# Moving five pieces of side work between the places of an attention turn: one projection in two halves, two transposes into one place, one more projection in two halves

## The chip, the cores and the metric

The kernel runs on one core of a Trainium2 chip. The metric is the device time of one launch in microseconds (us). The five engines of the core appear under their profile names: PE (TensorE, with its weight loads as PEld), DVE (VectorE), ACT (ScalarE), POOL (GpSimd) and SP (SyncE, which here only issues DMAs).

## The reference

A layer of attention and a mixture of experts, both modulated by a condition vector, over 4 batches of 512 tokens of width 256, all in float32.

```python
h = _layernorm(x) * (1 + ca) + sa
x = x + ga * _L0_attn_ref(h, wq, wk, wv, wo)      # 16 heads of 16, softmax over 512 keys
h = _layernorm(x) * (1 + cb) + sb
x = x + gb * _L0_ffn_ref(h, ...)                  # 32 experts of 96, top 4 of 32, plus a shared expert of 512
```

## The kernel before

**Stages.** After a short lead (loads, first projections, maxima of the first scores) come four attention turns, one for each batch (t.b = 0 to 3), then the rest of the second batch-wise work (`finish`), then the experts in 48 pairs of tiles, then the sums. The change touches the turns alone.

**A turn** has 32 *places*, 8 for each of 4 groups of 4 heads. At each place PE issues first the **score block**: two transposed score matmuls (`scoreT`, L863), whose exponentials ACT takes (L691), and two plain score matmuls (`score`, L834) of a later group, whose row maxima DVE takes (L1201). After the block comes `between`, the side work of the place. At every even place `between` begins with `values` (L876), the product of the exponentials and V, for a four of units. The remaining side work is laid out by hand in the tables `FIRST` (turn 0), `MIDDLE` (turns 1 and 2) and `LAST` (turn 3): name and place, or two places where a job is issued in two halves.

**The jobs** that matter here:
- `QK0` to `QK3` (L812) project the next batch's queries (even numbers) and keys (odd). A whole one is two matmuls, one for each half of the contraction; PE's records count four. ACT copies the result to `qk_raw` (L588), and SP spreads it to `q_rows` or `k_rows` by 8 DMAs (L356).
- `MAX0` to `MAX3` (L842) transpose the collected maxima of a group. ACT writes their negative to `neg_max` (L606), and SP puts that into a row of `q_rows` by 4 DMAs (L364). The next group's `scoreT` needs it, at the next place that is a multiple of 8.
- `HT0`, `HT1` (L798, inputs `h_even` or `h_odd`) are four transposes each of the previous batch's second normalisation. ACT writes them to `h2T` (L631) with scale and bias.
- `V0`, `V1` (L821), `WO0`, `WO1` (L889), `LOG` (L919), `RANK`, `NT0`, `NT1` are the rest.

**One side bank.** In turns 0 to 2 every one of these jobs writes the same PSUM bank (semaphores misc0_full and misc0_free). `claim` lets PE start a job only when the reader of the job before it has freed the bank; so the order of names in the table is the order of uses of the bank. ACT and DVE do their parts in their own `between`, after the two exponentials or maxima of that same place. There are three banks for transposed scores and three for plain ones, so the second `scoreT` of a block waits for an exponential of the block before, and the second `score` for a maximum of it.

Of the kernel before, what the change touches and what calls it, by code (L numbers as in the profile page):

```python
# [52 lines left out]
class Turn:  # L53
# [4 lines left out]
    LEAD = ("TP0", "TP1", "QK0", "QK1", "QK2", "QK3", "V0", "V1", "MAX3")  # L58

    FIRST = {"MAX0": 0, "TP0": 1, "TP1": 3, "QK0": 5, "QK1": 7, "MAX1": 8, "MOD0": 9, "MOD1": 11, "V0": (13, 15),  # L60
             "MAX2": 16, "MODT": 17, "QK2": (19, 21), "QK3": 23, "MAX3": 24, "V1": (27, 29), "NT0": 30, "NT1": 31}

    MIDDLE = {"MAX0": 0, "QK0": 1, "WO0": 3, "WO1": 5, "MAX1": 8, "QK1": 9, "V0": (11, 13), "HT0": 14, "HT1": 15,
              "MAX2": 16, "LOG": 17, "QK2": (19, 21), "QK3": 23, "MAX3": 24, "RANK": 25, "V1": (27, 29), "NT0": 30, "NT1": 31}

    LAST = {"MAX0": 0, "WO0": 3, "WO1": 5, "MAX1": 8, "HT0": 12, "HT1": 13, "LOG": 15, "MAX2": 16, "RANK": 20}
# [85 lines left out]
def adaln_moe_kernel(nc, x_in, wq, wk, wv, wo, gate, up, down, sgate, sup, sdown, c_in, wmod_in, out):  # L152
    ctx = ExitStack()
    with ctx:
# [403 lines left out]
        def _(act):  # L558
# [22 lines left out]
            def raw_qk(t, c):  # L581

                src = full(act, t, f"QK{c}")
                if c == 0:

                    for g in range(NG):
                        above(act, rows_ld[g], 128 * (t.b + 1))
                frees(act.activation(qk_raw[:, c, :], src, ACT.Copy), t, f"QK{c}")  # L588
# [12 lines left out]
            def negate_max(t, g):  # L601

                src = full(act, t, f"MAX{g}")

                above(act, maxrow, 64 * (NG * t.b + g + 1))
                frees(act.activation(neg_max[:, :], src[0:TJ * G, 0:P], ACT.Copy, scale=-1.0), t, f"MAX{g}")  # L606
# [49 lines left out]

            def between(t, place):

                if t.att and place % 8 == 0 and (place < 24 or t.pre):
                    negate_max(t, place // 8)  # L660
                for k in range(KD):
                    if t.at(f"TP{k}", place):
                        to_hT(t, f"TP{k}", t.b + 1)
                    if t.at(f"NT{k}", place):
                        to_hT(t, f"NT{k}", t.b + 2)
                    if t.at(f"V{k}", place):
                        values_out(t, k)
                    if t.at(f"HT{k}", place):
                        h2T_out(t, k)
                for c in range(4):  # L670
                    if t.at(f"QK{c}", place):
                        raw_qk(t, c)
                if t.next and place in (18, 20, 22, 26):
                    normalise(turn_of[t.b + 1], [(18, 20, 22, 26).index(place)])
                if t.post:
                    norms = t.WHEN_LAST["NORM"] if t.fill else t.WHEN["NORM"]
                    if place in norms:
                        second_norm(t, [j for j in range(TJ) if norms[j] == place])
                    if t.at("LOG", place):
                        logits_out(t)  # L680
                    if t.now("EXPS", place):
                        expert_weights(t)
# [92 lines left out]
        def _(pe):  # L775
# [61 lines left out]
            def turn_max(t, g):  # L837


                pe.wait_ge(max_done, 64 * t.b + 16 * g + 32)  # L840
                bank = claim(t, f"MAX{g}")
                filled(pe.transpose(bank[0:TJ * G, 0:P], max_q[:, (g + 1) % 2, :, :].rearrange("p q i -> p (q i)"), ident[:, :]), t, f"MAX{g}")  # L842
# [120 lines left out]
            def between(t, place):  # L963

                g = place // 8
                if place % 2 == 0:
                    if place % 8:
                        values(t.b, g, place // 2 % 4 - 1)
                    elif g or t.post:
                        values(t.b if g else t.b - 1, (g - 1) % NG, TJ - 1)  # L970
                if place % 8 == 0 and (g < 3 or t.pre):
                    turn_max(t, g)
                for k in range(KD):
                    if t.at(f"TP{k}", place):
                        tokens_to_columns(t, f"TP{k}", t.b + 1)
                    if t.at(f"NT{k}", place):
                        tokens_to_columns(t, f"NT{k}", t.b + 2)
                    if t.halves(f"V{k}", place):
                        project_v(t, k, t.halves(f"V{k}", place))
                    if t.at(f"MOD{k}", place):  # L980
                        modulate(t, k)
                    if t.at(f"WO{k}", place):
                        project_o(t, k)
                    if t.at(f"HT{k}", place):
                        pe.wait_ge(h2_norm, TJ * t.b)
                        rows_to_columns(t, f"HT{k}", h2[(t.b - 1) % 2], k)
                for c in range(4):
                    if t.halves(f"QK{c}", place):
                        project_qk(t, c, t.halves(f"QK{c}", place))
                if t.at("MODT", place):  # L990
                    modulation_columns(t)
                if t.at("LOG", place):
                    logits(t)
                if t.at("RANK", place):
                    ranks(t)
# [644 lines left out]
```

## Time and profile before

| | us |
|---|---|
| median of 3 runs | 603.67 (603.39 to 603.87) |
| the profiled execution | 604.01 |
| its span in the trace | 602.2 |

What lies around the span is 604.01 - 602.2 = 1.8 us. A row of the chain of waits gives a start, a length and what ran; it says what each moment of the end time was spent on. A block that runs unhindered is four pieces of 0.63, 0.01, 0.42 and 0.01 us in that view. In a row of the timeline the length is that of the merged instructions, and the bracket behind it says how long the engine sat idle before them and for whom. The turns lie between about 49 and 333 us.

### The profile page before, as it was taken

The numbers are of one execution on the slowest core, as the hardware profiler recorded it, in microseconds if no ns is written. First come the engines' busy times: TensorE is split into PE (matmuls) and PEld (weight loads), VectorE is DVE, ScalarE is ACT, GpSimd is POOL, SyncE is SP. The second block draws the span as 40 slices with busy tenths as digits, with TensorE's granted clock in tenths as the row PEclk, the third lists the DMA queues.
The fourth block names the chain that finished last, engine by engine and source line by source line (L and its number), as shares of the span: only waits on it lengthen the run. The fifth ranks groups of instructions, "written<-read, shape, count | busy, mean of one in ns | idle before, by whom it ended". The sixth has DMA issues, their size and how long they took to land.

```text
span 602.2 us, 10736 instructions
## 1 busy us (share of the span) xinstructions
PE 563.6 (94%) x3118; PEld 313.8 (52%) x3119; DVE 370.8 (62%) x860; ACT 255.3 (42%) x519; POOL 217.8 (36%) x284
## 2 busy tenths in 40 slices
PE   4889999999999999999999999998999999999881
PEld 3443233333333333333343465668888898897570
DVE  6385677778589785898855569435444444443683
ACT  3113545564765647555568140022343443433000
POOL 6100000000110751108434653441675666667332
PEclk9966999999999999999999999999999999999996
DMA  7242126100501224012101169524555645540791
GB/s 227 42 132 97 34 54 188 37 11 10 115 4 34 93 70 115 7 31 90 53 1 41 66 267 330 147 82 130 158 157 151 182 144 165 166 124 9 269 371 58
DMA packets 42343, 67.18 MB, mean 112 GB/s; under 512 B 9291, under 2 KB 32212, under 8 KB 41948
## 3 DMA queue, kind: packets, MB, share of 16 engines
q1 hardware_dynamic: 30208, 45.62, 25.9%
q0 software_dynamic: 7680, 16.87, 8.2%
q10 hardware_dynamic: 4416, 4.20, 2.1%
q8 instruction: 21, 0.34, 0.2%
q14 instruction: 18, 0.15, 0.1%
HBM read 38.93 MB, written 27.51 MB: 110 GB/s over the span
## 4 chain that ended last, share of the span: by engine, by line
PE 81%; DVE 8%; issue 3%; DMA 3%; SPq 1%; ACT 1%; POOL 1%; ACTq 0%; POOLq 0%; DVEq 0%
PE ps L863 23%; PE ps L876 10%; PE ps L1089 9%; PE ps L1110 6%; PE ps L960 6%; PE ps L812 5%; PE ps L954 3%; PE ps L834 3%; PE ps L1075 3%; PE ps L821 3%; PE ps L889 3%; DVE max_q L1201 2%; PE ps L1100 2%; PE ps L798 2%; PE ps L919 1%
## 5 line engine op out<-in xcount | busy, mean ns | idle before, releaser
L1201 DVE TENSOR_REDUCE max_q<-ps 128x1 f32<-128x512 f32 x256 | 163.8, 686 | 74.5 <-PE ps L834 72.8
L691 ACT ACTIVATE probs<-ps 128x512 f32<-128x512 f32 x256 | 138.0, 596 | 99.5 <-PE ps L863 99.2
L834 PE MATMUL ps<-k_rows,q_rows 31*128 31x512 f32 x512 | 149.7, 678 | 1.8 <-DMA k_rows<-qk_raw 1.8
L863 PE MATMUL ps<-q_rows,k_rows 32*128 32x512 f32 x512 | 147.6, 646 | 0.9 <-DVE max_q L1201 0.9
L545 POOL DMA_INDIRECT results<-y_sb,dest x96 | 94.5, 984 | 64.8 <-issue 35.0
L863 PEld LDWEIGHTS ps<-q_rows,k_rows 32*128 32x128 f32 x512 | 42.9, 186 | 71.6 <-ACT probs L691 52.2
L1089 PE MATMUL ps<-up_sb,oT 128*128 x384 | 70.7, 328 | 1.5 <-DVE oT L1565 1.3
L876 PE MATMUL ps<-probs,v_ext 128*32 128x512 f32 x512 | 68.2, 605 | 1.1 <-ACT probs L691 1.1
L1089 PEld LDWEIGHTS ps<-up_sb,oT 128*128 128x128 f32 x384 | 61.4, 191 | 2.1 <-issue 1.9
L1110 PE MATMUL ps<-down_sb,e_hidT 96*128 x192 | 49.8, 383 | 3.8 <-ACT e_hidT L748 3.8
L498 POOL TENSOR_TENSOR rstd<-veps,mhalf 128x4 f32<-128x4 f32 x4 | 4.1, 1036 | 134.3 <-DVE veps L1283 132.4
L1565 DVE COPY oT<-ps 128x512 f32<-128x512 f32 x48 | 33.1, 691 | 30.0 <-PE ps L1075 30.0
L834 PEld LDWEIGHTS ps<-k_rows,q_rows 31*128 31x128 f32 x512 | 46.0, 194 | 10.5 <-DVE max_q L1201 3.9
L1572 DVE CAST dest<-xe 128x2 int32<-128x2 f32 x48 | 14.8, 309 | 48.4 <-ACT e_silu L731 46.5
L731 ACT ACTIVATE e_silu<-ps 128x192 f32<-128x192 f32 x48 | 15.8, 330 | 63.6 <-PE ps L1089 63.6
L740 ACT ACTIVATE y_sb<-ps 128x512 f32<-128x512 f32 x48 | 28.7, 597 | 29.2 <-PE ps L1110 27.0
L1110 PEld LDWEIGHTS ps<-down_sb,e_hidT 96*128 96x128 f32 x192 | 32.7, 190 | 7.7 <-issue 5.1
L876 PEld LDWEIGHTS ps<-probs,v_ext 128*32 128x32 f32 x512 | 10.1, 108 | 49.8 <-issue 31.1
L644 ACT ACTIVATE sh_tanh<-ps 128x512 f32<-128x512 f32 x16 | 9.6, 597 | 61.5 <-PE ps L960 61.5
L525 POOL DMA_INDIRECT dispatched<-h_even,slot_i x32 | 31.4, 983 | 9.5 <-POOL h_even L524 9.5
L525 POOL DMA_INDIRECT dispatched<-h_odd,slot_i x32 | 31.1, 972 | 9.1 <-POOL h_odd L524 9.1
L1075 PE MATMUL ps<-ident,xe 128*128 128x128 f32 x192 | 29.0, 273 | 0.8 <-DMA xe<-dispatched 0.8
(180 smaller groups left out, 695.7 us busy)
## 6 DMA issues: line engine op xcount, KB each, us to landing
xe<-dispatched SPq DMA_DIRECT2D x96, 129.0 KB, 2.1
up_sb<-results SPq DMA_DIRECT2D x16, 512.0 KB, 7.9
up_sb<-in_up SPq DMA_DIRECT2D x2, 3072.0 KB, 15.1
dispatched<-pad_rows SPq DMA_DIRECT2D x33, 129.0 KB, 4.5
down_sb<-in_down SPq DMA_DIRECT2D x1, 3072.0 KB, 31.3
x<-in_x ACTq DMA_DIRECT2D x4, 512.0 KB, 5.1
q_rows<-qk_raw SPq DMA_DIRECT2D x64, 32.0 KB, 1.9
k_rows<-qk_raw SPq DMA_DIRECT2D x64, 32.0 KB, 1.9
```

The lines of the kernel that those rows point to most:

```text
L525: pool.indirect_dma_start(out=xs, out_offset=bass.IndirectOffsetOnAxis(ap=slot_i[:, TOPK * j + k:TOPK * j + k + 1], axis=0), in_=h2[p % 2] ...
L545: pool.indirect_dma_start(out=yk, out_offset=bass.IndirectOffsetOnAxis(ap=dest[:, n:n + 1], axis=0), in_=y_sb[:, n % (2 * YP), :], in_offs ...
L691: act.activation(probs[:, u % 8, :], ps[:, st_bank(t.b, g, u), :], ACT.Exp).then_inc(exp_done, 1)
L834: pe.matmul(ps[:, banks[u % len(banks)], :], q_rows[32 * i:32 * i + ONE, b % 2, g, qt * P:(qt + 1) * P], k_rows[32 * i:32 * i + ONE, b % 2 ...
L863: pe.matmul(ps[:, st_bank(b, g, n), :], k_rows[32 * i:32 * i + 32, b % 2, g, kt * P:(kt + 1) * P], q_rows[32 * i:32 * i + 32, b % 2, g, :] ...
L876: mm = pe.matmul(ps[32 * i:32 * i + 32, O, :], v_ext[:, b % 2, kt, head(g, i), :], probs[:, (4 * kt + i) % 8, :], start=(kt == 0), stop=(k ...
L960: mm = pe.matmul(bank, w[:, k, c * P:(c + 1) * P], h2_columns(s, k), start=(k == 0), stop=(k == KD - 1))
L1075: mm = pe.transpose(ps[:, r % 2, (2 * half + k) * P:(2 * half + k + 1) * P], xe[:, 2 * r + half, k * P:(k + 1) * P], ident[:, :])
L1089: mm = pe.matmul(ps[:, 2 + r % 2, 2 * DM * half:2 * DM * (half + 1)], xeT[:, r % 2, (2 * half + k) * P:(2 * half + k + 1) * P], up_sb[:, b ...
L1110: mm = pe.matmul(ps[:, 6 + r % 2, half * D:(half + 1) * D], e_hidT[:, r % 2, half * P:(half + 1) * P], down_sb[:, bass.ds(es[half] * D, D) ...
L1201: dve.tensor_reduce(max_q[:, g % 2, qt, i:i + 1], ps[:, banks[(16 * g + n) % len(banks)], :], AXX, ALU.max).then_inc(max_done, 1)
L1565: dve.tensor_copy(xeT[:, r % 2, :], ps[:, r % 2, :]).then_inc(t_done, 1)
```

## The change

Two tables change, and `between` of ACT and of PE handles `MAX1` and `MAX3` after the projections of the same place instead of ahead of them, so that the order of uses of the bank stays that of the tables.

```diff
@@ -58,9 +58,9 @@
     FIRST = {"MAX0": 0, "TP0": 1, "TP1": 3, "QK0": 5, "QK1": 7, "MAX1": 8, "MOD0": 9, "MOD1": 11, "V0": (13, 15),
-             "MAX2": 16, "MODT": 17, "QK2": (19, 21), "QK3": 23, "MAX3": 24, "V1": (27, 29), "NT0": 30, "NT1": 31}
-
-    MIDDLE = {"MAX0": 0, "QK0": 1, "WO0": 3, "WO1": 5, "MAX1": 8, "QK1": 9, "V0": (11, 13), "HT0": 14, "HT1": 15,
+             "MAX2": 16, "MODT": 17, "QK2": (19, 21), "QK3": (23, 25), "MAX3": 25, "V1": (27, 29), "NT0": 30, "NT1": 31}
+
+    MIDDLE = {"MAX0": 0, "QK0": 1, "WO0": 3, "WO1": 5, "QK1": (7, 9), "MAX1": 9, "V0": (11, 13), "HT0": 15, "HT1": 15,
@@ -656,8 +656,9 @@
-                if t.att and place % 8 == 0 and (place < 24 or t.pre):
-                    negate_max(t, place // 8)
+                for g in (0, 2):
+                    if t.at(f"MAX{g}", place):
+                        negate_max(t, g)
@@ -670,6 +671,9 @@
+                for g in (1, 3):
+                    if t.at(f"MAX{g}", place):
+                        negate_max(t, g)
@@ -968,8 +972,9 @@
-                if place % 8 == 0 and (g < 3 or t.pre):
-                    turn_max(t, g)
+                for m in (0, 2):
+                    if t.at(f"MAX{m}", place):
+                        turn_max(t, m)
@@ -987,6 +992,9 @@
+                for m in (1, 3):
+                    if t.at(f"MAX{m}", place):
+                        turn_max(t, m)
```

`LAST` is as it was, and so is the rest of `MIDDLE`, whose `QK3` stays whole at 23 and `MAX3` at 24.

In the rows of order below, the numbers of lines behind L are those of each kernel: L863, L834, L876, L842, L812 and L798 of before are L867, L838, L880, L846, L816 and L802 of after.

PE, turn 1, places 7 to 9 and the start of 10, before:

```order
L863 MATMUL ps<-q_rows,k_rows 128x512 x2
L834 MATMUL ps<-k_rows,q_rows 128x512 x2
L863 MATMUL ps<-q_rows,k_rows 128x512 x2
L834 MATMUL ps<-k_rows,q_rows 128x512 x2
L876 MATMUL ps<-probs,v_ext 32x512 x4
L842 MATMUL ps<-ident,max_q 16x128
L863 MATMUL ps<-q_rows,k_rows 128x512 x2
L834 MATMUL ps<-k_rows,q_rows 128x512 x2
L812 MATMUL ps<-hT,wk_sb 128x512 x2
L863 MATMUL ps<-q_rows,k_rows 128x512 x2
```

The same places after:

```order
L867 MATMUL ps<-q_rows,k_rows 128x512 x2
L838 MATMUL ps<-k_rows,q_rows 128x512 x2
L816 MATMUL ps<-hT,wk_sb 128x512
L867 MATMUL ps<-q_rows,k_rows 128x512 x2
L838 MATMUL ps<-k_rows,q_rows 128x512 x2
L880 MATMUL ps<-probs,v_ext 32x512 x4
L867 MATMUL ps<-q_rows,k_rows 128x512 x2
L838 MATMUL ps<-k_rows,q_rows 128x512 x2
L816 MATMUL ps<-hT,wk_sb 128x512
L846 MATMUL ps<-ident,max_q 16x128
L867 MATMUL ps<-q_rows,k_rows 128x512 x2
```

Half of the key projection stands at place 7, which held a score block alone; the turning of the maxima stands right behind the other half, with no block in between. Turn 2 reads the same, and in turn 0 the same rows stand at places 23 to 25.

PE, turn 1, places 14 and 15, with the semaphores waited for, before:

```order
L876 MATMUL ps<-probs,v_ext 32x512 [waits exp_done]
L876 MATMUL ps<-probs,v_ext 32x512 x3
L798 MATMUL ps<-ident,h_even 128x128 [waits misc0_free,h2_norm]
L798 MATMUL ps<-ident,h_even 128x128 x3
L863 MATMUL ps<-q_rows,k_rows 128x512 [waits exp_done] x2
L834 MATMUL ps<-k_rows,q_rows 128x512 [waits max_done] x2
L798 MATMUL ps<-ident,h_even 128x128 [waits misc0_free,h2_norm]
L798 MATMUL ps<-ident,h_even 128x128 x3
```

After:

```order
L880 MATMUL ps<-probs,v_ext 32x512 [waits exp_done]
L880 MATMUL ps<-probs,v_ext 32x512 x3
L867 MATMUL ps<-q_rows,k_rows 128x512 [waits exp_done] x2
L838 MATMUL ps<-k_rows,q_rows 128x512 [waits max_done] x2
L802 MATMUL ps<-ident,h_even 128x128 [waits misc0_free,h2_norm]
L802 MATMUL ps<-ident,h_even 128x128 x3
L802 MATMUL ps<-ident,h_even 128x128 [waits misc0_free,h2_norm]
L802 MATMUL ps<-ident,h_even 128x128 x3
```

The score block that stood between the two fours of transposes now stands ahead of both, and the second four waits for the bank right behind the first.

ACT, turn 1, from place 14 to the start of 17, before:

```order
L691 ACTIVATE probs<-ps 128x512 x2
L631 ACTIVATE h2T<-ps,modT 128x512
L691 ACTIVATE probs<-ps 128x512 x2
L631 ACTIVATE h2T<-ps,modT 128x512
L691 ACTIVATE probs<-ps 128x512 x2
L606 ACTIVATE neg_max<-ps 16x128
L691 ACTIVATE probs<-ps 128x512 x2
```

After:

```order
L695 ACTIVATE probs<-ps 128x512 x4
L631 ACTIVATE h2T<-ps,modT 128x512 x2
L695 ACTIVATE probs<-ps 128x512 x2
L606 ACTIVATE neg_max<-ps 16x128
L695 ACTIVATE probs<-ps 128x512 x2
```

Both copies of the transposes stand behind the exponentials of place 15.

## Rows read from the trace of the kernel before

**Rows 1.** The page: share of busy time, granted clock in 40 slices, chain by engine.

```profile
PE 563.6 (94%) x3118; PEld 313.8 (52%) x3119; DVE 370.8 (62%) x860; ACT 255.3 (42%) x519; POOL 217.8 (36%) x284
...
PEclk9966999999999999999999999999999999999996
...
PE 81%; DVE 8%; issue 3%; DMA 3%; SPq 1%; ACT 1%; POOL 1%; ACTq 0%; POOLq 0%; DVEq 0%
```

**Rows 2.** Chain of waits (start, length, what), turn 1, places 7 to 10.

```profile
143.66 0.63 PE ps L863 x2
...
144.73 1.36 PE ps L863 x3
...
146.70 0.99 PE ps L876 x8
147.70 0.21 PE ps L842
147.91 0.63 PE ps L863 x2
...
148.98 1.91 PE ps L812 x4
150.89 0.63 PE ps L863 x2
```

**Rows 3.** Chain of waits, turn 1, places 14 to 17.

```profile
160.36 1.00 PE ps L876 x8
161.35 0.59 PE ps L798 x4
161.94 0.63 PE ps L863 x2
...
163.01 0.59 PE ps L798 x4
163.60 1.20 PE ps L863 x4
...
165.68 0.99 PE ps L876 x8
166.67 0.21 PE ps L842
166.88 0.63 PE ps L863 x2
```

**Rows 4.** Chain of waits, turn 1, place 19: a projection in halves.

```profile
172.99 1.06 PE ps L812 x2
175.12 1.00 PE ps L876 x8
```

**Rows 5.** Timeline, ACT (idle before it in brackets), turn 1, places 15 and 9.

```profile
163.03 1.09 ACT L691 ACTIVATE probs<-ps 128x512 f32<-128x512 f32 x2 [0.27 <-PE ps L863]
...
164.00 0.78 ACT L631 ACTIVATE h2T<-ps,modT 128x512 f32<-128x512 f32 x1
```

```profile
150.93 0.60 ACT L588 ACTIVATE qk_raw<-ps 128x512 f32<-128x512 f32 x1 [0.85 <-PE ps L812]
```

**Rows 6.** Timeline, end of turn 3: PE takes up after a wait for ACT.

```profile
330.70 2.06 ACT L691 ACTIVATE probs<-ps 128x512 f32<-128x512 f32 x4 [0.70 <-PE ps L863]
...
332.81 1.06 PE L876 MATMUL ps<-probs,v_ext 128*32 128x512 f32 x8 [1.14 <-ACT probs L691]
```

**Rows 7.** Chain of waits in the lead: hand-over from ACT to PE, at the low clock.

```profile
12.87 0.79 ACT hT L578
13.66 0.25 issue
13.90 3.76 PE ps L812 x4
```

**Rows 8.** Stretches: sum, busy time by engine, granted clock; turn 0 places 23 to 26 and turn 1 places 14 to 16.

```profile
159.29:166.88 7.59, 7.59 (x53) 2.64 (x53) 4.11 (x7) 5.69 (x11) 2.97 (x3) 1.00 0.69 134
106.95:114.18 7.23, 7.23 (x41) 2.40 (x45) 4.59 (x8) 4.76 (x10) 0.00 (x0) 1.00 0.23 49
```

**Rows 9.** Timeline, SP's DMA issues in turn 0 around place 24 and in turn 1.

```profile
110.29 5.01 SPq L356 DMA_DIRECT2D k_rows<-qk_raw  x8
115.34 14.96 SPq L364 DMA_DIRECT2D q_rows<-neg_max  x7
...
156.55 5.52 SPq L379 DMA_DIRECT2D dispatched<-pad_rows  x11
```

## The prediction

> **What bounds the kernel now.** I read the page first, then the chain of waits through turns 0 to 2, then the timeline at the places that change. On the page PE is busy 94% of the span and holds 81% of the chain [rows 1]. That share is an average, so the question is what a place of a turn costs. The chain answers it. A score block that is not held up takes 1.07 us (161.94 to 163.01) [rows 3]. To it comes the side work: 0.99 for values, 0.59 for four transposes, 1.06 for half a projection, 1.91 for a whole one, 0.21 for a turning of maxima [rows 2 to 4]. A place that holds enough is plain PE work, for instance half a projection and a block, 172.99 to 175.12 = 2.13 us [rows 4]. A place that holds nothing but the block isn't cheaper by the missing work: the block at place 7 begins at 143.66, place 8's begins at 144.73, and that one lasts until 146.70 = 1.97 us where it would take 1.07 [rows 2]. The first half of it waits for the exponentials and maxima of the block before. So an empty odd place costs 1.07 + 0.90, and there is a **floor** of about 1.97 us from block start to block start. The same happens behind place 15: after HT1 the block of place 16 takes 163.60 to 165.68 = 2.08 us, 1.01 too much, since ACT still has two exponentials and a copy to do for place 15 [rows 3, 5]. And in turn 0 place 25 is empty; places 23 to 26 take 7.23 us in all [rows 8], as the stretch of turn 1 does (143.66 to 150.89).
>
> **Part one: the projection in halves and the maxima behind it (turn 1 and 2 places 7 to 9, turn 0 places 23 to 25; three times).** Before: block 1.07, nothing, block 1.97, values 0.99, maxima 0.21, block 1.07, whole projection 1.91, sum 7.23 (143.66 to 150.89) [rows 2]. What goes: 0.90 of waiting in place 8's block, because half a projection (1.06) now stands ahead of it and covers ACT and DVE. What is moved: half of 1.91, at a price of 1.06 for a half, so 2 x 1.06 - 1.91 = 0.21 more PE time. What is new: the maxima's transpose sits right behind the second half on the same bank. PE is in order, so it and all of the following block wait until ACT has copied the projection. Count from T, the end of place 9's block. ACT starts its two exponentials about 0.02 after the block's end and could start a third instruction 0.97 after that (163.03 to 164.00) [rows 5], so it is free at T + 0.99. The half projection ends at T + 1.06, and the copy begins 0.04 after the projection's end (148.98 + 1.91 = 150.89, copy 150.93) and takes 0.60 [rows 2, 5]: it ends at T + 1.70. PE takes up 0.05 after ACT's end (330.70 + 2.06 = 332.76, PE 332.81) [rows 6]. With no matmul under way the weight load of the transpose isn't hidden; I put 0.08 for it, between 0 (the modelled start of the matmul in that same row) and 0.2. Then 0.21. The next block starts at T + 2.04. After: 1.07 + 1.06 + 1.07 + 0.99 + 1.07 + 2.04 = 7.30 against 7.23, **+0.07 each, +0.2 for three**. For turn 0 the same sum begins behind place 22 and ends with the freed block of place 26: 1.06 + 1.07 + 0.99 + 1.07 + 2.04 + 1.07 = 7.30 against 7.23 [rows 8].
>
> **Part two: both transposes at 15 (turns 1 and 2).** Before, from 160.36: values 0.99, HT0 0.59, block 1.07, HT1 0.59, block 2.08, values 0.99, maxima 0.21, which is 166.88 [rows 3]. After: values 0.99 (161.35), block 1.07 (162.42), and from there, again T: HT0 ends at T + 0.59, but ACT has the exponentials of place 15 first, so the copy of HT0 runs from T + 0.99 to T + 1.77 (0.78) [rows 5]; PE takes up at T + 1.82, the weight load adds 0.1, HT1 takes 0.59: T + 2.51. That is 1.33 us of PE standing still where before a block lay in between. What comes back is the 1.01 of place 16: the exponentials of place 15 ended long ago, so its block takes 1.07. Then values and maxima: 162.42 + 2.51 + 1.07 + 0.99 + 0.21 = 167.20 against 166.88, **+0.32 each, +0.6 for two**. HT1's copy ends at T + 3.3, ahead of the claim by MAX2 at T + 4.6, so nothing else is held.
>
> **What costs nothing, and what covers it.** MAX1's row goes to SP about 3 us later than before; its use is at place 16, some 14 us on. Behind it SP issues the 8 DMAs of QK1 and 11 pads, which end at 162.1 (156.55 + 5.52) [rows 9] and would now end near 164; MAX2's rows are wanted at 167.2. In turn 0 QK3's 8 DMAs (5.0 us) start near 113 instead of 110.29 and end near 118; MAX3's four (some 2.2 us) follow by 120.2 and have landed near 122.5. The block that needs them, turn 1's first, is at 125.8 (7.30 - 7.23 later now), so cover of 3 us is left; if SP's queue were 3 us later still, turn 1 would start late by the excess. POOL's scaling of `h_even` waits for HT1 and starts 1.4 us later, and then waits for DVE's slots for far longer than that. DVE reads nothing that is moved.
>
> **The sum.** 3 x 0.07 + 2 x 0.32 = 0.85, call it +0.9 us. Made against the profiled execution (span 602.2, with 1.8 around it, 604.01) that is 604.9; that execution lay 0.34 above the median of 603.67, and against the median it is **604.6**.
>
> **A rule weighed.** The trace shows what a side job costs when its reader is elsewhere: in rows 3 the copy of HT0 lies under the block of place 15, and PE has no gap there. The Trainium skill ("Perfetto Trace Analysis", Matmuls) says that independent groups should rotate through different PSUM banks so that the evacuation of one overlaps the matmuls of the next. Part two does the opposite, two groups in a row on one bank. By that rule alone the two pairs would be 2 x 1.33 us worse; the rows give 1.01 of each back.
>
> **Rivals.**
> *Longer pauses, clearly slower.* Five pauses on the one bank are made (three of about 0.8, two of 1.3 us). My hand-over of 0.05 is from one row; in the lead the step from ACT to PE took 0.25 (13.66 to 13.90) [rows 7], though at the low clock. With 0.25 and an unhidden weight load of 0.2, each pause grows by about 0.3: 5 x 0.3 = 1.5 on top of 0.9, that is 606.1. It decides early: 0.07 us more in each pause puts the sum over 0.2%.
> *Shorter pauses, a gain.* If the pause behind the half projections did not exist, part one would be 0.78 better each (T + 1.27 in place of T + 2.04, so -0.7 each, -2.1 in all) and, with part two as above, the time 602.4. Against it: the claim is in program order, the copy lies behind two exponentials, and nothing in rows 5 lets ACT start sooner. It would need ACT's exponentials to begin before the block's modelled end, by 0.8 us. Half of that (602.5 to 604.2, no change) is easier to believe.
> *The clock falls in the pauses.* The granted clock is full level (2.4 GHz) from slice 5 until the last one, and over the stretch with place 16's wait it is 1.00 [rows 1, 8], so pauses of 0.9 to 1.0 us haven't lowered it; 1.3 us is new. If it fell to the other level (1.2 GHz) for one place after each pause, four records of projection would take 3.76 as in the lead and not 1.91 [rows 2, 7]; that is some 2 us for each of five places, +10, 614.6. The Trainium skill ("TensorE: Matmul & The Clock Gate", A second HAM failure mode: psum-queue depth-cycling) tells of a kernel in which micro-idles between groups of matmuls made the clock go to and fro; by that rule this would be the outcome.
>
> **How the numbers follow.** The forecast as summed, 604.2 to 604.9: 0.46. Longer pauses, 604.9 to 607: 0.37. Shorter ones, 602.5 to 604.2: 0.09. A gain, below 602.5: 0.06. The clock: 0.02. The median can be told from no change by about 0.2%, 1.2 us, so the first case and the third are "same" (604.9 is just that bound), which gives 0.55; slower is 0.39, faster 0.06. The range for 8 in 10 leaves out the gain, the lower part of the shorter pauses, the top of the longer ones and the clock: 603.4 to 606.6.
>
> **What would show it.** In the chain of the changed kernel: place 8's block 1.07 us instead of 1.97 in turns 1 and 2, and place 26's in turn 0; place 16's 1.07 instead of 2.08. PE idle ahead of the maxima's transpose for about 0.7 to 0.8 us on ACT's `qk_raw`, three times, and ahead of the second four of transposes for about 1.3 us on ACT's `h2T`, twice. Places 7 to 9 sum to 7.30, places 14 to 16 (from the values on) to 6.8. If a block after a pause is still over 1.5 us, the floor was not what I take it for, and the time is 606 or more. If the start of turn 1 waits on a DMA, the cover on SP was misjudged.

## The result, and the profile after

The changed kernel takes **607.84 us** (median of 6 runs, 606.72 to 608.91), the kernel before 603.70 us beside it (603.39 to 604.21, 6 runs). The ratio is 1.0069 with a 95% interval of [1.0055, 1.0084]: slower by 4.1 us, where 0.9 was forecast, and outside the range of 603.4 to 606.6.

The profiled execution took 608.85 us with a span of 607.1, which is 4.9 more than the span of before. The page of after, in the parts that answer to [rows 1]:

```profile
PE 562.3 (93%) x3118; PEld 312.1 (51%) x3119; DVE 370.8 (61%) x860; ACT 255.4 (42%) x519; POOL 217.9 (36%) x284
...
PEclk9976998999999999999999999998999999999996
...
PE 74%; DVE 7%; DMA 6%; issue 4%; POOL 3%; ACT 3%; SPq 2%; POOLq 0%; ACTq 0%; DVEq 0%
```

PE's busy time is 1.3 us lower than before (562.3 against 563.6) and the span 4.9 longer. Two 8s stand in the row of the granted clock where before had 9 throughout: slice 7 (91 to 106 us) and slice 28 (410 to 425 us). Neither lies at a place that the diff touches.

**The changed places.** The chain of waits of after, turn 1, places 7 to 10 (start, length, what), beside [rows 2]:

```profile
144.80 0.63 PE ps L867 x2
...
145.87 1.06 PE ps L816 x2
...
149.64 0.47 PE ps L867 x2
150.10 1.06 ACT probs L695 x2
151.17 0.60 ACT qk_raw L588
151.76 0.14 issue
151.90 0.27 PE ps L846
152.17 0.63 PE ps L867 x2
```

Place 8's block, 1.97 us long before, now takes its 1.07 (values start at 148.00). The block of place 9 ends at about 150.06, and the next starts at 152.17: the maxima wait for the exponentials, then for the copy of the projection. From block 7 to block 10 it is 7.37 us against 7.23, +0.14. The same chain at places 14 to 17, beside [rows 3]:

```profile
161.63 1.00 PE ps L880 x8
162.63 0.63 PE ps L867 x2
...
164.69 0.79 ACT h2T L631
165.48 0.14 issue
165.62 0.63 PE ps L802 x4
166.24 0.63 PE ps L867 x2
...
167.31 0.99 PE ps L880 x8
168.31 0.21 PE ps L846
168.52 0.63 PE ps L867 x2
```

That is 6.89 us against 6.52 (160.36 to 166.88), +0.36 in unrounded times. PE stands still until 165.62, and the block of place 16 takes 1.07 (166.24 to 167.31) where it took 2.08. The timeline of PE has both pauses, with their lengths and what ended them:

```profile
151.90 0.27 PE L846 MATMUL ps<-ident,max_q 128*16 128x128 f32 x1 [0.78 <-ACT qk_raw L588]
...
165.62 0.63 PE L802 MATMUL ps<-ident,h_even 128*128 128x128 f32 x4 [1.32 <-ACT h2T L631]
```

The other three of the five read the same (0.78 twice, 1.33 once).

**The two stretches of low clock.** The chain of after right behind `MODT` of turn 0, ahead of every changed place:

```profile
95.86 1.72 PE ps L880 x8
97.57 1.15 PE ps L867 x2
```

Values take 1.72 where the same work takes 1.00 at 161.63. The second is at the start of the experts. The timeline of PE (the bracket is the idle time ahead, and for whom), of before:

```profile
408.47 0.66 PE L1075 MATMUL ps<-ident,xe 128*128 128x128 f32 x4 [0.33 <-DMA xe<-dispatched]
410.45 1.56 PE L1089 MATMUL ps<-up_sb,oT 128*128 x8 [1.33 <-DVE oT L1565]
```

and of after:

```profile
411.00 0.66 PE L1083 MATMUL ps<-ident,xe 128*128 128x128 f32 x4 [0.73 <-DMA xe<-dispatched]
412.58 2.12 PE L1097 MATMUL ps<-up_sb,oT 128*128 x8 [0.93 <-DVE oT L1573]
414.50 1.06 PE L1083 MATMUL ps<-ident,xe 128*128 128x128 f32 x4
```

The gaps ahead are 1.66 us in both (0.33 + 1.33, 0.73 + 0.93), and the instructions are the same. Only the lengths behind them differ. The stretches, from the start of the first up-projection to that of the third (length, then busy time of five engines; PEclk is the number behind POOL's), of before and of after, and of after around 96:

```profile
410.45:414.25 3.80, 3.80 (x27) 3.74 (x28) 1.66 (x7) 0.79 (x3) 0.00 (x0) 1.00 0.47 118
```

```profile
95.80:100.20 4.40, 4.40 (x22) 0.96 (x18) 2.48 (x5) 2.18 (x5) 0.00 (x0) 0.61 0.86 140
...
412.58:418.05 5.47, 5.47 (x27) 5.29 (x27) 1.66 (x7) 0.79 (x3) 0.00 (x0) 0.69 0.44 110
```

5.47 against 3.80 is +1.67 at the experts' start. In rows of 0.1 us the granted clock is 0.50, the level of 1.2 GHz, from 96.0 to 99.4 and from 413.4 to 416.8, 3.4 us each time.

**Where the 4.9 us of this execution came from**, by the starts of the same work in both traces:

| step | us |
|---|---|
| lead: 17.1 us at low clock instead of 20.5 (the place of a values block: 60.35 to 59.71) | -0.64 |
| low clock at 96 (the lateness before place 23 of turn 0, less the line above) | +1.64 |
| turns: 3 x 0.14 and 2 x 0.36 (the values of turn 3's place 2 start at 282.00 instead of 279.86, in all +2.14 with the two lines above) | +1.14 |
| low clock at the experts' start | +1.67 |
| one wait for `xe` in the experts is 1.37 instead of 0.48 | +0.89 |
| the rest | +0.2 |

The wait in the second last line, before and after:

```profile
449.50 0.66 PE L1075 MATMUL ps<-ident,xe 128*128 128x128 f32 x4 [0.48 <-DMA xe<-dispatched]
```

```profile
454.09 0.66 PE L1083 MATMUL ps<-ident,xe 128*128 128x128 f32 x4 [1.37 <-DMA xe<-dispatched]
```

So the turns explain 1.1 us, and the question is what the low clock has to do with the change.

### The profile page after: what moved, and what is told of

It is laid out like the page before. It is cut to its first block, busy times and chain, and to the rows that moved or that the text cites. A ratio compares the mean times of both kernels' runs of the same rounds, so it can differ in the third digit from the quotient of the medians.

```text
span 607.1 us, 10736 instructions
## 1 busy us (share of the span) xinstructions
PE 562.3 (93%) x3118; PEld 312.1 (51%) x3119; DVE 370.8 (61%) x860; ACT 255.4 (42%) x519; POOL 217.9 (36%) x284
## 4 chain that ended last, share of the span: by engine, by line
PE 74%; DVE 7%; DMA 6%; issue 4%; POOL 3%; ACT 3%; SPq 2%; POOLq 0%; ACTq 0%; DVEq 0%
PE ps L867 22%; PE ps L880 10%; PE ps L1097 9%; PE ps L1118 6%; PE ps L816 4%; PE ps L1083 3%; DMA dispatched<-h_odd,slot_i 3%; PE ps L825 3%; PE ps L893 2%; DVE max_q L1209 2%; PE ps L838 2%; PE ps L964 2%; POOL dispatched L525 2%; PE ps L1108 2%; PE ps L802 1%
## 5 line engine op out<-in xcount | busy, mean ns | idle before, releaser
L838 PE MATMUL ps<-k_rows,q_rows 31*128 31x512 f32 x512 | 149.8, 676 | 1.9 <-DMA k_rows<-qk_raw 1.9
L867 PE MATMUL ps<-q_rows,k_rows 32*128 32x512 f32 x512 | 146.5, 652 | 0.9 <-DVE max_q L1209 0.9
L867 PEld LDWEIGHTS ps<-q_rows,k_rows 32*128 32x128 f32 x512 | 41.8, 187 | 73.0 <-ACT probs L695 53.7
L1097 PE MATMUL ps<-up_sb,oT 128*128 x384 | 72.1, 332 | 1.2 <-DVE oT L1573 0.9
L880 PE MATMUL ps<-probs,v_ext 128*32 128x512 f32 x512 | 68.9, 610 | 1.1 <-ACT probs L695 1.1
L838 PEld LDWEIGHTS ps<-k_rows,q_rows 31*128 31x128 f32 x512 | 45.4, 192 | 9.0 <-DVE max_q L1209 3.9
L880 PEld LDWEIGHTS ps<-probs,v_ext 128*32 128x32 f32 x512 | 10.1, 108 | 50.1 <-issue 35.1
```

The costliest lines, as they stand in the source:

```text
L838: pe.matmul(ps[:, banks[u % len(banks)], :], q_rows[32 * i:32 * i + ONE, b % 2, g, qt * P:(qt + 1) * P], k_rows[32 * i:32 * i + ONE, b % 2 ...
L867: pe.matmul(ps[:, st_bank(b, g, n), :], k_rows[32 * i:32 * i + 32, b % 2, g, kt * P:(kt + 1) * P], q_rows[32 * i:32 * i + 32, b % 2, g, :] ...
L880: mm = pe.matmul(ps[32 * i:32 * i + 32, O, :], v_ext[:, b % 2, kt, head(g, i), :], probs[:, (4 * kt + i) % 8, :], start=(kt == 0), stop=(k ...
L1097: mm = pe.matmul(ps[:, 2 + r % 2, 2 * DM * half:2 * DM * (half + 1)], xeT[:, r % 2, (2 * half + k) * P:(2 * half + k + 1) * P], up_sb[:, b ...
```

## The experiments

Two theories. **Pauses:** the change's five pauses of PE in the turns make the chip lower the clock, there or later. **Moment:** the pauses only make everything behind them later, and whether the clock falls at a gap that both kernels have hangs on the moment at which it comes.

Each timed execution lists its mean granted clock, and executions of one kernel fall into groups by it. Of the 95 of the kernel before that stood beside the runs at 603 to 605 us below, 48 are at 0.977 or more with a median of 603.4, 15 at 0.975 or 0.976 with 604.8, and 32 lower with 606.2. A stretch of 3.4 us at half clock is 0.003 of the mean. I call the first group *undisturbed*; it lets the work of two kernels be compared with little of the clock in it.

The mean doesn't say where the time at half clock lies. In the traces the lead alone has 17.1, 20.5 or 23.9 us of it. The trace of before has a mean of 0.974 with 20.5 us in the lead and no stretch behind it, and took 604.0; three of the 32 in the lowest group took 603.9 and look like it. So the counts below say how often an execution has little low clock, and only a trace says whether it fell at the experts' start.

### The parts, beside a kernel before of 652 us

`e1_again` is the changed kernel, unchanged. `e2_ht15` has part two alone:

```diff
-    MIDDLE = {..., "HT0": 14, "HT1": 15,
+    MIDDLE = {..., "HT0": 15, "HT1": 15,
```

`e3_qk12` has the halves and the maxima behind them in turns 1 and 2 alone (`"QK1": (7, 9), "MAX1": 9`), `e4_qk0` in turn 0 alone (`"QK3": (23, 25), "MAX3": 25`), both with the new order of the maxima's handling. `e5_late` is the kernel before with one more matmul in turn 1, whose result is overwritten:

```diff
                 w = (wq_sb, wk_sb)[c % 2]
+                if t.b == 1 and c == 1:
+                    for _ in range(1):
+                        pe.matmul(bank, w[:, 0, (c // 2) * P:(c // 2 + 1) * P], hT[:, 0, :], start=True, stop=True)
                 for k in halves:
```

> The changed kernel once more, for its spread and for a second trace. Theory S (sum plus clock): the turns cost 1.1 us as in the first trace (3 x 0.13 and 2 x 0.36), and the other 2 to 4 us come from stretches of some 3 us at half the granted clock, outside the changed places, at other times in this trace than at 96 and 413 us; time 606.7 to 608.9, with steps between runs. Theory L (lateness): the turns end 2.1 us late again and the experts start late for want of their first tiles; no low-clock stretch is needed, and the time is the same in all runs.

> Only both transposes at 15 in turns 1 and 2. Theory S: turns +0.7 (2 x 0.36), and the rest of the change's loss if pauses of 1.3 us are what lets the clock fall: 604.4 without low-clock stretches, 606 to 608 with them. Theory L: +0.7 of lateness gives a share of the 4.1 in proportion, some 606.3.

> Only QK1 in halves at 7 and 9 with MAX1 behind it, turns 1 and 2. Theory S: turns +0.26, no pause over 0.8 us: 604.0 and no low-clock stretch in the turns. Theory L: +0.26 of lateness, 604.7.

> Only QK3 in halves at 23 and 25 with MAX3 behind it, turn 0. Theory S: +0.13, 603.8 and the trace as before. Theory L: 604.2.

> The kernel before with one extra matmul ahead of QK1 in turn 1: the first half of the projection is done twice, its first result overwritten. It is pure PE time of 0.86 us with no new wait. Theory P (phase of the clock): any shift of the later program by about a microsecond moves its thin spots (after the modulation's tiny matmuls, at the start of the experts) against the chip's clock decisions, so the time rises by 0.9 plus 0 to 3.5 us, in steps near 1.7, and the trace shows stretches of 3.4 us at half clock. Theory W (the pauses of the change do it): no pause is added here, so 604.6 and no low stretch. Theory L (a late chain of scatters): +0.9 of lateness in the turns gives a rise in proportion to the change's 4.1 for 1.1, some +3.3, without low clock.

Here the kernel before took 652.5 us (655.5 beside `e5_late`), with single executions some 5 us around it. The five took 654.4, 654.1, 652.3, 653.7 and 654.9; the ratios are 1.0019 [0.9989, 1.0049], 1.0045 [1.0002, 1.0087], 0.9995 [0.9952, 1.0037], 1.0005 [0.9965, 1.0045] and 0.9984 [0.9933, 1.0035]. The trace of `e1_again` has a stretch at half clock from 218 to 228 us that no trace at 603 has. Differences of 1 us can't be told there, and these runs settle nothing. Of the five ratios only that of part two alone, 1.0045, lies above 1 with its whole interval.

### Before and after again, part two alone, lateness alone, the gap filled

Beside the next runs the kernel before takes 603.6 to 603.8. `e6_before` is the kernel before, unchanged; `e7_after`, `e8_ht15` and `e9_late` are the kernels of `e1_again`, `e2_ht15` and `e5_late`. `e10_fill` is the changed kernel with two matmuls of 512 columns more at the experts' start, one on each side of the second transposes of `xe`, into a bank that the next projection overwrites:

```diff
+                    if begun is None and r == 1:
+                        pe.matmul(ps[:, 7, :], ident[:, :], sup_sb[:, 0, :], start=True, stop=True)
                     if more:
                         turn_rows(i, q, r)
+                    if begun is None and r == 1:
+                        pe.matmul(ps[:, 7, :], ident[:, :], sup_sb[:, 0, :], start=True, stop=True)
```

> The kernel before, unchanged, as a control for the clock. Theory P (phase): the kernel before has thin spots too, and in a second trace it may show low-clock stretches of 3.4 us at other places than the lead and the end. Theory W (the pauses of the change cause them): none between 55 us and the last 15 us, as in the first trace.

> The changed kernel again, on a chip where the kernel before takes 603.6 us. Theory P (phase of the clock): 604.8 at best, and spread up to 609 in steps of some 1.7, the trace with low-clock stretches at other times than 96 and 413 us. Theory W (the pauses cause low clock): always above 606.5. The stretches of the changed places cost 0.13 (three) and 0.36 (two) whatever the total.

> Only both transposes at 15 in turns 1 and 2. Sum from the traces: +0.72, so 604.3 if nothing else is lost; theory W expects the two long pauses of 1.3 us to carry most of the change's 4.1, so 606.5 to 607; theory P expects 604.3 plus a share that has nothing to do with the pauses.

> The kernel before with one matmul (0.86 us) done twice ahead of QK1 in turn 1: lateness of 0.9 us without any pause. Theory P: 604.5 plus the same kind of excess as the changed kernel, up to 607.5. Theory W: 604.5 and no excess. Theory L (a late chain of scatters makes the excess): 604.5 plus some 2.

> The changed kernel with two extra matmuls of 0.85 us at the start of the experts, in the two gaps in which PE waits for the second pair of tiles and for DVE's first copy (0.73 and 0.93 us in its trace). Theory P: with PE busy there the clock no longer falls at 413 us, so 1.5 us better than the changed kernel on this chip, 606 or less. Theory W: no change, since the clock falls for the pauses in the turns; theory L: no change or 0.8 worse.

**The kernel before has the stretch at 96 as well.** `e6_before` took 603.88 (603.32 to 606.2, 8 runs; 603.58 beside it), and its traced execution is the one of 606.2. Its chain behind `MODT`:

```profile
96.67 1.81 PE ps L876 x8
98.49 1.15 PE ps L863 x2
```

So that stretch isn't made by the change: it comes in some executions of either kernel.

`e7_after` took 606.91 (604.94 to 609.02, 10 runs) against 603.77, ratio 1.0046 [1.0022, 1.0069]. With the first result, **none of the changed kernel's 16 executions is undisturbed**, where half of those of before are. Its group of 0.975 to 0.976 has a median of 606.7 (8 executions): 603.4 + 1.1 for the turns + 1.7 for one stretch are 606.2. One execution, 604.94 at 0.974, lies where the trace of before would with 1.1 us more (604.0 at 0.974), so not every one of the 16 need have fallen at the experts' start. The trace of `e7_after` has the stretch at the experts' start (412.3) and none at 96.

`e8_ht15` took 605.36, ratio 1.0004 [0.9982, 1.0026]; four of ten undisturbed, at 604.0, which is 0.6 more than before where 2 x 0.36 = 0.7 was due. `e9_late`, without a single pause, took 605.27, ratio 1.0014 [0.9992, 1.0035]; four of ten undisturbed, at 604.1, 0.7 above before, where 0.87 (1.06 + 1.72 - 1.91) more work was put in. `e10_fill` took 606.52, ratio 1.0031 [1.0008, 1.0053]; four of ten are undisturbed, at 604.9. Its trace at the filled gap:

```profile
411.00 1.02 PE L1137 MATMUL ps<-sup_sb,ident 128*128 128x512 f32 x2
...
412.30 1.02 PE L1141 MATMUL ps<-sup_sb,ident 128*128 128x512 f32 x2
413.48 1.56 PE L1097 MATMUL ps<-up_sb,oT 128*128 x8 [0.16 <-issue]
```

1.56, full clock, behind a gap of 0.16 us. The pauses in the turns are those of after, and yet undisturbed executions are back. That speaks against pauses as the cause of the fall at the experts' start, and for the gap. It is one trace and four executions; the median of 606.52 is 0.4 below that of `e7_after`, and not the 606 or less that was expected.

### A microsecond late without a pause, the pauses taken away, part one alone, before filled

`e11_late11` is `e9_late` with a second, narrower matmul behind the first, 1.07 us in all. `e12_apart` keeps the halves and puts a place between each pair on the one bank:

```diff
-    FIRST = {..., "QK3": (23, 25), "MAX3": 25, ...
+    FIRST = {..., "QK3": (23, 25), "MAX3": 26, ...
-    MIDDLE = {..., "QK1": (7, 9), "MAX1": 9, "V0": (11, 13), "HT0": 15, "HT1": 15,
+    MIDDLE = {..., "QK1": (7, 9), "MAX1": 10, "V0": (11, 13), "HT0": 14, "HT1": 15,
```

`e13_qk3` is part one in all three turns, without part two (`"HT0": 14`). `e14_fillb` is the kernel before with the two matmuls of `e10_fill`.

> The kernel before with PE held 1.07 us longer in turn 1 (one full and one quarter matmul done twice ahead of QK1), so the turns end about as late as with the change, and no pause is added. Theory P (lateness against the chip's clock decisions): as with the changed kernel hardly any run above a mean clock of 0.976, a low-clock stretch near 413 us in the trace, median 606 to 607. Theory W (the pauses, or what the change does to the turns, make the low stretch): some half of the runs at 0.977 or more as in the kernel before, median 604.9.

> The halves kept, the pause taken away: QK1 in halves at 7 and 9 with MAX1 at 10 (turns 1 and 2), QK3 in halves at 23 and 25 with MAX3 at 26 (turn 0), HT0 and HT1 at 14 and 15 as before. If the sum is right, each of the three saves 0.70 (7.23 becomes 1.07 + 1.06 + 1.07 + 0.99 + 1.07 + 1.06 + 0.21 = 6.53), so the turns end 2.1 us earlier than in the kernel before, and a run without low clock between the lead and the end takes 601.3 where the kernel before takes 603.4. If the even place 10 needs the time for itself, 0.2 each less.

> Part one alone, all three (turn 0 at 23 and 25, turns 1 and 2 at 7 and 9, the maxima right behind), HT0 and HT1 as before. Sum: 3 x 0.13 = +0.4; runs of a mean clock of 0.977 or more take 603.8. Theory P: some of the runs lie at that clock, since the shift is small; theory W: three pauses of 0.75 us, so fewer than with the transposes alone.

> The kernel before with the two extra matmuls at the start of the experts, the control for the fill in the changed kernel. Theory P: the start of the experts seldom brings a low stretch in the kernel before, so the fill gains nothing and costs up to 0.5: 603.7 to 604.2 in median, and as many runs at a clock of 0.974 or less as in the kernel before (those come from about 96 us). If the gap at the experts' start matters in the kernel before too, 603.0.

Beside them the kernel before took 603.99 (34 runs, 16 undisturbed at 603.4).

| | median | ratio | undisturbed | their median |
|---|---|---|---|---|
| `e11_late11` | 606.88 | 1.0028 [1.0009, 1.0047] | 2 of 12 | 605.4 |
| `e12_apart` | 602.74 | 0.9976 [0.9958, 0.9994] | 0 of 12 | |
| `e13_qk3` | 604.10 | 0.9994 [0.9977, 1.0011] | 9 of 12 | 604.0 |
| `e14_fillb` | 604.39 | 1.0001 [0.9982, 1.0021] | 7 of 12 | 603.9 |

**Lateness alone brings the stretch.** `e11_late11` makes no pause: its chain in turn 1 shows the old wait of place 8 and then plain work.

```profile
146.32 1.36 PE ps L867 x3
...
150.57 1.06 PE ps L813 x2
151.62 0.22 PE ps L814 x2
151.84 1.72 PE ps L816 x4
```

The extra work is 1.09 us by these rows (1.06 + 0.22 + 1.72 against 1.91), and the medians lie 2.9 apart. The ratio is weaker, 1.7 us with 0.5 to 2.8 as its interval, which doesn't exclude the bare 1.09. The trace has the clock at half level from 413.7, as after has. All three had been expected of a fall that hangs on the moment: a median of 606 to 607, hardly an undisturbed execution, a stretch near 413.

**Part one alone.** In `e13_qk3` the chain of turn 1 has the pause of after:

```profile
149.33 0.60 ACT qk_raw L588
149.93 0.14 issue
150.06 0.27 PE ps L846
150.33 0.63 PE ps L867 x2
```

Block 7 begins at 142.97, and to 150.33 it is 7.36, +0.13 by these rows, three times 0.4. The undisturbed executions are 0.6 above before's, and there are nine of them in twelve, against 16 of 34 beside them: a kernel with three of the five pauses shows no more low clock than the kernel before. The two longer pauses alone (`e8_ht15`) left four of ten.

**The pauses taken away.** In `e12_apart` the chain of turn 1, from block 7 to block 10:

```profile
141.98 0.63 PE ps L867 x2
...
143.05 1.06 PE ps L816 x2
...
147.24 1.06 PE ps L816 x2
148.30 0.63 PE ps L867 x2
```

6.32 us, and 0.21 for the maxima a place later (150.37): 6.53 against 7.23, no wait left, 0.7 us better each. Turn 3 starts 2.1 us earlier than before once the lead is taken out. But the median gains only 1.3 us on before, and no execution is undisturbed. The timeline shows why:

```profile
405.68 0.66 PE L1083 MATMUL ps<-ident,xe 128*128 128x128 f32 x4 [0.62 <-DMA xe<-dispatched]
407.40 2.61 PE L1097 MATMUL ps<-up_sb,oT 128*128 x8 [1.06 <-DVE oT L1573]
```

The gap is 1.68 us, as long as in after (1.66), and the clock falls in it, without a pause of the change anywhere and with everything early instead of late. So "the later, the worse" falls as well; of the theories here, what is left is the moment. It makes a prediction that sounds absurd: give this kernel a microsecond more of work and it shouldn't get slower.

### More work for the fastest edition

`e16_apart_late` and `e18_apart_late` are `e12_apart` with the matmuls of `e11_late11` ahead of the first half of `QK1` in turn 1:

```diff
+                if t.b == 1 and c == 1 and 0 in halves:
+                    for _ in range(1):
+                        pe.matmul(bank, w[:, 0, (c // 2) * P:(c // 2 + 1) * P], hT[:, 0, :], start=True, stop=True)
+                        pe.matmul(bank[:, 0:P], w[:, 0, (c // 2) * P:(c // 2 + 1) * P], hT[:, 0, 0:P], start=True, stop=True)
```

`e15_apart_fill` is `e12_apart` with the matmuls of `e10_fill`, `e17_apart_again` is `e12_apart` once more.

> The edition with the pauses taken away (maxima at 10 and 26, transposes at 14 and 15) plus the two extra 512 wide matmuls in the gaps of PE at the start of the experts, which cost 0.3 to 0.5 us where no stretch of low clock is. Theory (the first gap of the experts is where the clock falls, and whether it does hangs on the moment at which the gap comes): the stretch at 407 is gone, its 1.6 us come back, and the median is 602.7 - 1.6 + 0.4 = 601.5, with most executions at a mean clock of 0.977 or more. Rival (the low clock of that edition comes from somewhere else): mean clock as before at 0.976, median 603.1.

> The same edition, with 1.07 us of extra matmuls in turn 1 (at place 7), which make everything behind them 1.07 us later and touch neither a pause nor the start of the experts. Theory (the moment decides): the gap at the experts' start comes near where it does in the kernel with part one alone, which never showed a stretch there, so it mostly stays at full clock: median 602.7 + 1.07 - 1.6 = 602.2, less than that of the edition with less work. Rival (the fall at the experts' start belongs to this edition whatever the moment): 602.7 + 1.07 = 603.8.

> The edition with the pauses taken away once more, beside the two others and on the same chip: 602.7, all executions at a mean clock of 0.976 or less, by either theory.

> The same kernel as in the run before (pauses taken away, 1.07 us of extra matmuls in turn 1), hoped for on a chip that runs at full clock through the turns. Theory (the moment of the gap decides whether the clock falls at the experts' start): mostly no stretch there, median near 602.7 + 1.07 - 1.6 = 602.2, a good part of the executions at a mean clock of 0.977 or more. Rival (the fall belongs to this edition whatever the moment): 603.8, none of them at 0.977 or more.

Beside the first three the kernel before took 658.02 and no execution had a mean clock over 0.962: 656.51, 0.9967 [0.9926, 1.0007]; 658.24, 1.0004 [0.9975, 1.0032]; 656.28, 0.9973 [0.9947, 1.0]. The last agrees with the gain of `e12_apart` there (0.9976); otherwise they are inconclusive, and the filled edition was never measured beside a kernel before of 604. The record names the chip of these three by the same number as that of `e7_after` to `e14_fillb`, minutes earlier and at 604, so what makes the 658 is open.

Beside `e18_apart_late` the kernel before took 604.98 (13 runs, 4 undisturbed). It took 603.60 (601.83 to 605.29, 10 runs), ratio 0.9979 [0.996, 0.9999]. **Five of ten are undisturbed, at 602.25**, where `e12_apart` had none of twelve. The trace:

```profile
406.41 0.66 PE L1087 MATMUL ps<-ident,xe 128*128 128x128 f32 x4 [0.15 <-DMA xe<-dispatched]
408.56 1.56 PE L1101 MATMUL ps<-up_sb,oT 128*128 x8 [1.50 <-DVE oT L1577]
```

A gap of 1.65 us, and full clock behind it. The median missed the 602.2 of the expectation and lies nearer to the rival's 603.8. Before itself is 1.0 us slower here than beside `e12_apart` (604.98 against 603.99), and the other half of the executions has a lower mean clock, as those of before do. The second thing that the rival expected, none undisturbed, is out, and these five are 0.5 us faster than `e12_apart`'s usual 602.7, with 1.07 us more work. The ratios to before are nearly the same (0.9979 and 0.9976), but each is known to 0.002 either way, and the extra microsecond is 0.0018: the medians can't say whether it was free.

**The moments side by side.** The low clock of the lead ends somewhere between 53 and 59 us in the traces. From there to the start of the first up-projection, that is the end of the gap, in all traces taken beside a kernel before of 603 to 605 us:

| trace | us from the lead's last low clock to the gap's end | clock at the gap |
|---|---|---|
| `e8_ht15` | 354.07 | falls |
| `e11_late11` | 354.44 | falls |
| `e12_apart` | 354.63 | falls |
| before | 355.06 | stays |
| `e18_apart_late` | 355.53 | stays |
| `e6_before` | 356.51 | stays |
| `e13_qk3` | 356.95 | stays |
| `e9_late` | 357.34 | stays |
| `e7_after` | 357.38 | falls |
| after | 357.54 | falls |
| `e14_fillb`, filled | 356.53 | stays |
| `e10_fill`, filled | 357.57 | stays |

(From 410.45 - 55.39 for before, 412.58 - 55.04 for after, and so on.) The falls lie in two bands with 2.7 us between them in which none fell, and the length of the gap doesn't order them: it is 1.66 in `e8_ht15` and after, and also in before and `e13_qk3`. Where it fell, it fell 0.4 to 1.0 us behind the gap's end. Filled, the gap at the moment of after's (357.57 and 357.54) leaves the clock alone. The table was made after the runs, and the upper band begins between two traces that are only 0.04 us apart (`e9_late`, `e7_after`).

The stretch at 96 sorts in the same way, over all twelve traces. The last matmul of `MODT` ends 39.75 to 39.88 us after the lead's last low clock in the five that have the stretch (`e6_before`, after, `e9_late`, `e10_fill`, `e14_fillb`). It ends at 40.04 in before, at 38.3 in two and at 41.2 to 41.7 in the last four, and none of these has it.

## Why the prediction was wrong

**Right, by the rows.** The floor: place 8's block 1.07 instead of 1.97 and place 16's 1.07 instead of 2.08. Both pauses: PE idle 0.78 us ahead of the maxima's transpose and 1.3 us ahead of the second transposes, for the instructions named. The start of turn 1 waits for no DMA, so the cover on SP held. The Trainium skill's rule that groups should rotate through banks ("Perfetto Trace Analysis", Matmuls) has the right sign here; of the 1.33 us for each pair that the prediction worked out from its rows for that rule, a net 0.36 is left in the trace. And the direction of every local term: halves a little worse, transposes worse, although PE's busy time fell.

**A little small.** Part one was put at +0.07 and measured +0.14, part two at +0.32 and +0.36. The step is the hand-over from ACT to PE: 0.05 was taken from one row in [rows 6], the rows now say 0.14 ("issue" behind `qk_raw` and `h2T`), and the maxima's matmul with its weight load in the open takes 0.27 where I had 0.21 + 0.08. For the transposes my 0.05 + 0.1 gave the right start, T + 1.92; they take 0.63 in the chain where I had 0.59. Together the turns cost 1.14 and not 0.85: against the median of before that is 604.8, well inside the range. The five pauses weren't longer by 0.3 each, so the rival of longer pauses, on whose side the sign fell, was wrong in its mechanism. (The rival of a gain adds up to 602.2 by its own terms, 603.67 - 2.1 + 0.6, and not to 602.4; nothing hangs on it.)

**What failed** is the silent step under all cases, that what lies behind the turns is only shifted and costs nothing; with it the rival of the clock, at 0.02, was looked for at the wrong places. I looked for a fall in the pauses that the change makes, found full clock over the waits of before [rows 8], and stopped. Those waits lie inside score blocks, with PE busy for 7.59 of 7.59 us, so they say nothing of idle pauses. In the pauses the clock indeed never fell, in any of the five traces that have them (603 to 609 us). The Trainium skill ("TensorE: Matmul & The Clock Gate", A second HAM failure mode: psum-queue depth-cycling) tells of a kernel in which frequent micro-idles between groups of matmuls made the clock go to and fro; here those of up to 1.3 us among 0.6 to 2 us of work brought none. But two places that the change doesn't touch are on the edge in both kernels: behind `MODT` (8 matmuls of 4 columns, 16 records) at 96 us, and the gaps at the experts' start. [Rows 1] showed only one execution, in which neither fell; 47 of 95 executions of before have a lower mean clock than the undisturbed ones, and take 1.4 to 2.8 us longer in the median. With the change the second place fell in both traces of the changed kernel, and no execution of it had the mean clock of an undisturbed one. That is worth 1.7 us, against a whole forecast of 0.9. A wait for `xe` near 450 us comes on top in some traces: 0.62 to 1.37 in four of the five with a fall, 0.48 (before) and 0.93 (`e18_apart_late`) in two of the five without.

**Shown and not shown.** Shown: the cost of each part in the turns (trace of after, `e13_qk3`, `e8_ht15`); that the stretch at the experts' start costs 1.67 us for the same matmuls; that it needs no pause (traces of `e11_late11`, `e12_apart`). That it goes with a microsecond of lateness rests on `e12_apart` and `e18_apart_late` (none of twelve and five of ten undisturbed, and one trace each); in the other direction, `e11_late11`'s two of twelve against 16 of 34 can still be chance. That it needs the gap rests on one trace and four executions of `e10_fill`. Argued from mean clocks alone: which stretch the untraced executions have, and so how much of the median's 4.1 us each stretch makes. Open: what fixes the moments, what makes some runs 652 to 658 us, why the wait for `xe` grows, and 0.4 us of after's 606.7 that the sum 603.4 + 1.1 + 1.7 leaves.

## What to carry to other kernels

Halving a job to fill an empty slot is worth its full gain only if the next user of its bank stands at least one block behind: with the maxima one place later the same halves gained 0.7 us each instead of losing 0.14, and the kernel was 0.24% faster than before [0.06%, 0.42%] instead of slower. When a change shifts all later work by a microsecond, look in the rest of the trace for gaps of PE next to narrow or small matmuls, for here they turned a shift into 1.7 us; and before blaming an edit for 2 us, run a kernel that is only late by as much. One trace of before is one draw: compare executions of equal mean clock, and let a trace say where the low clock lies.

## What the runs showed of the hardware

- PE idle for 1.65 to 1.69 us, in two pieces with 0.66 us of transposes between them, was followed by 3.4 us at half clock in five traces (after, `e7_after`, `e8_ht15`, `e11_late11`, `e12_apart`) and by full clock in four (before, `e9_late`, `e13_qk3`, `e18_apart_late`). It costs 5.47 us against 3.80 for the same 27 matmul records.
- PE idle for 0.78 us (three times) and 1.3 us (twice) between dense groups of matmuls in the turns left the clock at full level (after, `e7_after`, `e10_fill`; `e8_ht15` and `e13_qk3` for their part).
- With 1.07 us of useless matmuls in turn 1 five of ten executions have a mean clock of 0.977 or more (`e18_apart_late`), without them none of twelve (`e12_apart`); the ratios to before, 0.9979 [0.996, 0.9999] and 0.9976 [0.9958, 0.9994], can't tell the two apart.
- The lead's low clock ends between 53 and 59 us, with 17.1, 20.5 or 23.9 us at half clock in it, from trace to trace of similar kernels.
- The same program takes 604 us in some runs and 652 to 658 in others, even under one chip number within minutes. In the long ones the turns have stretches of 3.4 to 13.7 us at half clock, and PE is busy 90% of the span and not 94% (`e1_again`), so the clock is only part of it.
